# Moving an output projection and re-placing idle matrix products in a windowed-attention kernel

## The reference

```
scores = einsum('bhqd,bhkd->bhqk', q, k) * SCALE
scores = where(|query - key| <= 64, scores, -inf)
out = einsum('bhqk,bhkd->bhqd', softmax(scores), v)
out = out.transpose(0, 2, 1, 3).reshape(B, N, D) @ Wo + bo
```

## Time and profile before

| | |
|---|---|
| median of 3 runs | 2369.12 us (2367.04 to 2376.89) |
| profiled execution | 2362.09 us, span 2360.4 us from the first to the last instruction |
| mean granted TensorE clock | 0.983 |
| busy: PE, PEld, DVE, ACT, POOL | 96%, 90%, 79%, 60%, 12% |
| sampling phase | about 86 to 269 us of the span |
| attention phase | about 324 to 849 us |
| spline phase | about 849 us to the end |
| idle products (L1282) | 248 |

### The profile page before, as it was taken

The page is one execution under the profiler, slowest core; times in us unless marked ns, Lnnn a source line. Parts: engine busy times, 40 slices in busy tenths (PEclk is TensorE's granted clock), DMA queues, the critical chain, the costliest instruction groups (busy, mean ns, idle before and its releaser), DMA issues.

```text
span 2360.4 us, 49109 instructions
## 1 busy us (share of the span) xinstructions
PE 2264.6 (96%) x20033; PEld 2120.2 (90%) x20033; DVE 1873.1 (79%) x2241; ACT 1413.1 (60%) x1391; POOL 295.0 (12%) x169
## 2 busy tenths in 40 slices
PE   6599989999999899999999999999999999999999
PEld 5266777888888799999999999999999999999999
DVE  7699765666666588776776776679999999999996
ACT  6489303444444464534434435499998888888881
POOL 7622100000000022221321321000000000000000
PEclk9799998999999899999999999999999999999999
DMA  6656241111111111111111111221000000000000
GB/s 206 181 147 156 69 159 27 47 47 48 47 48 47 44 32 45 41 51 54 39 50 54 40 49 37 66 80 30 23 23 23 23 23 23 23 23 23 23 19 10
DMA packets 115455, 129.99 MB, mean 55 GB/s; under 512 B 17063, under 2 KB 106167, under 8 KB 115127
## 3 DMA queue, kind: packets, MB, share of 16 engines
q1 hardware_dynamic: 95215, 103.54, 14.6%
q10 hardware_dynamic: 16520, 14.34, 2.1%
q0 software_dynamic: 3616, 10.54, 1.7%
HBM read 92.79 MB, written 35.58 MB: 54 GB/s over the span
## 4 chain that ended last, share of the span: by engine, by line
PE 62%; DVE 2%; ACT 0%; issue 0%; DVEq 0%
PE spline_acc L1994 17%; PE spline_acc L1990 10%; PE spline_acc L1961 10%; PE spline_acc L1964 10%; PE spline_acc L1962 10%; PE spline_acc L1991 5%; PE spline_xT L764 0%; DVE spline_f_high L1725 0%; DVE spline_f L1725 0%; DVE spline_f_low L1725 0%; DVE spline_f L1714 0%; DVE spline_weights_split L1761 0%; DVE spline_b L1731 0%; DVE spline_front L1731 0%; DVE spline_b L803 0%; DVE spline_front L803 0%
## 5 line engine op out<-in xcount | busy, mean ns | idle before, releaser
L1961 PE MATMUL spline_acc<-spline_f,spline_weights_high 128*128 128x328 f32 x1536 | 481.2, 314 | 1.8 <-DVE spline_f L1714 1.8
L1962 PE MATMUL spline_acc<-spline_f,spline_weights_high 128*128 128x328 f32 x1536 | 479.0, 312 | 0.0
L1964 PE MATMUL spline_acc<-spline_f,spline_weights_low 128*128 128x328 f32 x1536 | 465.5, 312 | 0.0
L1994 PE MATMUL spline_acc<-spline_weights,spline_f 128*128 128x192 f32 x1968 | 342.5, 327 | 0.0
L1994 PEld LDWEIGHTS spline_acc<-spline_weights,spline_f 128*128 128x128 f32 x1968 | 316.6, 190 | 0.0
L1990 PE MATMUL spline_acc<-spline_weights_split,spline_f_high 128*128 128x384 f32 x984 | 304.9, 374 | 2.0 <-DVE spline_f L1725 2.0
L1961 PEld LDWEIGHTS spline_acc<-spline_f,spline_weights_high 128*128 128x128 f32 x1536 | 288.3, 188 | 2.2 <-DVE spline_f L1714 1.6
L1962 PEld LDWEIGHTS spline_acc<-spline_f,spline_weights_high 128*128 128x128 f32 x1536 | 288.8, 188 | 0.0
L1964 PEld LDWEIGHTS spline_acc<-spline_f,spline_weights_low 128*128 128x128 f32 x1536 | 286.0, 188 | 0.0
L1991 PE MATMUL spline_acc<-spline_weights_split,spline_f_low 128*128 128x192 f32 x984 | 248.5, 253 | 0.0
L1714 DVE SCALAR_TENSOR_TENSOR spline_f<-spline_front 128x984 fp32r<-128x984 f32 x128 | 150.3, 1215 | 88.7 <-PE spline_acc L1964 86.6
(11 more groups left out here) (240 smaller groups left out, 4924.5 us busy)
## 6 DMA issues: line engine op xcount, KB each, us to landing
spline_front<-pos_scr SPq DMA_DIRECT2D x32, 540.0 KB, 4.3
hid_scr<-spline_hid SPq DMA_DIRECT2D x64, 164.0 KB, 1.8
spline_xn<-hid_scr SPq DMA_DIRECT2D x41, 256.0 KB, 3.1
attend_spread<-rec_scr SPq DMA_DIRECT2D x128, 61.5 KB, 2.1
pix_scr<-spline_front SPq DMA_DIRECT2D x32, 225.0 KB, 3.1
spline_weights_raw<-w SPq DMA_DIRECT2D x1, 6144.0 KB, 21.5
spline_step_to<-w SPq DMA_DIRECT2D x36, 128.0 KB, 2.1
spline_step_from<-w SPq DMA_DIRECT2D x36, 128.0 KB, 2.1
```

The lines of the kernel that those rows point to most:

```text
L1961: nc.tensor.matmul(z, high, x_high, start=start, stop=False)
L1962: nc.tensor.matmul(z, high, x_low, start=False, stop=False)
L1964: last = nc.tensor.matmul(z, low, x_high, start=False, stop=stop)
L1994: last = nc.tensor.matmul(z, rest[:, cols], w2[:, i, r - SETS, :], start=False, stop=stop)
```

## The change

Four things change.

1. In `sample_phase` TensorE issues 70 products of the 128 x 128 identity with itself (fp32, 128 columns, result unread) before the first image.
2. `project_out` and `residual` of the second half move from `q = 0` to `q = 1`. On TensorE the projection then stands after the second quarter's `queries_scores` and before `keys_scores` of `q = 2`; on VectorE the addition stands after the second `maximum`. The first half's stay at `q = 0`.
3. The 4 idle products at `q = 1`, `i = 1` are gone from the 14 pairs after the first.
4. Idle products are added: in the first pair 24 for 18 at `q = 1`, `i = 0`, and 6 new ones at `q = 2`, `i = 1`, ahead of `queries_scores`; in the last pair 6 each at `q = 1`, `2` and `3` of the first half, ahead of `queries_scores`; in `finish` 6 after each of the two `keys_scores`, and 30 for 20 at its end.

```diff
@@ sample_phase, tensor
+            for _ in range(70):
+                nc.tensor.matmul(acc[:, 1, 1, 0:P], c.ident[:], c.ident[:], start=True, stop=True)
             for u in range(2):
                 image(0, u, True)
@@ attend_phase, vector, pair
-                        if q == 0 and not first:
+                        if q == i and not first:
                             residual(tt - 1 if u == 0 else tt, v, i, use(t, (Y_LAST if last else Y)[i]))
@@ attend_phase, tensor, finish
                 for c in range(2):
                     keys_scores(a, u, 1, c, use(t, MAX[0]))
+                    keep_going(6, xb[:, claim(use(t, MIX_LAST[1])), 0:HG * P])
                 for c in range(2):
                     mix(a, u, 1, c, use(t, MIX_LAST[1]))
                 project_out(a - 2, 1, use(t, Y_LAST[1]))
-                keep_going(20, tp[:, 0, 0:HG * P])
+                keep_going(30, tp[:, 0, 0:HG * P])
@@ attend_phase, tensor, pair
                         if first and q == 1 and i == 0:
-                            keep_going(18, xb[:, claim(use(t, X[0])), 0:HG * P])
-                        if q == 1 and i == 1 and more:
-                            keep_going(6 if first else 4, xb[:, claim(use(t, V[0])), 0:HG * P])
+                            keep_going(24, xb[:, claim(use(t, X[0])), 0:HG * P])
+                        if i == 0 and not more and q >= 1:
+                            keep_going(6, xb[:, claim(use(t, X[0])), 0:HG * P])
+                        if q == 1 and i == 1 and first:
+                            keep_going(6, xb[:, claim(use(t, V[0])), 0:HG * P])
+                        if first and q == 2 and i == 1:
+                            keep_going(6, xb[:, claim(use(t, V[0])), 0:HG * P])
                         if nxt:
                             queries_scores(a + 1, w, 1 - i, q)
-                        if q == 0 and not first:
+                        if q == i and not first:
                             project_out(a - 2, i, use(t, Y[i]))
```

## The result

The changed kernel takes 2389.59 us, the median of 12 runs (2377.50 to 2392.37), beside 2368.61 us for the kernel before, 12 runs on the same chip (2362.27 to 2376.89). The ratio is 1.0081, with a 95% interval from 1.0062 to 1.0099: slower by 21.0 us, where +28.6 was forecast. The profiled execution took 2391.96 us, with a span of 2390.3 and a granted clock of 0.981 over the whole of it (before: 2362.1 and 0.983).

The account below looks back on a forecast made before the run. TensorE, busy 96% of the span, was taken as the bound. 35 - 5.3 + 0.9 - 2.0 + 0 = +28.6 us on the median 2369.1 gave 2398 us; likeliest case 2381 to 2424, 8-in-10 range 2359 to 2428.

Parts of the forecast that it names:

- The steady pair's schedule: Second half of each of 14 steady pairs, clock held: idle products and one wait gone, a 1.23 us wait new, 0.0 us.
- ScalarE's cover: Steady pair: second exponential moves back 0.9 us, leaving 1.2 us of cover; rival that ScalarE becomes late: 2375 us, chance 0.05.
- The clock falls in steady pairs: Steady pair's second half: only 32-row products around a 1.2 us wait lower TensorE's clock; forecast case, chance 0.57.
- The rival in which the clock holds: Steady pairs: no falls because the gap is short and a full-array projection follows; sum -6.4, 2363 us, chance 0.27.
- How many, and how dear: Steady pairs: 9 of 14 fall at 3.85 us each, 35 us; ends 0 and 80.
- The rule of the Trainium skill: Steady pairs: only gaps more than twice as long lower the clock, so this term would be 0; kept as a rival.
- The first pair: First attention pair: added idle products thicken the stretch and remove its 5.7 us clock fall, net -5.3 (at worst +0.4).
- The last pair: Last attention pair and `finish`: added idle products cost 2.8, a held clock gives -1.9; net +0.9, between -2 and +5.
- The sampling: Sampling's first image: 70 products raise the clock and remove VectorE's waits of 1.30 and 1.61; -2.0, between -2.9 and +3.
- the forecast's longer case: Sampling's 70 products: each as long as an idle product of 384 columns, making 16 to 32 us in all.
- the clock's term: Steady pairs: cost of clock falls, 9 x 3.85 = 35 us.
- the rival of the 70 products: Sampling: the 70 products run over by 3 to 15 us, clock held; 2369 to 2381 us, chance 0.03 by itself.

## Why the prediction was nearly right, step by step

*The steady pair's schedule* (0.0 allowed 0.2): right. The wait is 1.16 for 1.23, the second quarter starts 2.03 after the first for 2.02, and with the clock held (four products back in the wait) the pair is 29.17 for 29.02. The step from the projection to the keys' scores was taken as 1.88, from the step to the idle products in the kernel before; it is 2.10 (535.61 to 537.71 there), enough for the 0.15. ScalarE's cover was enough: no wait stands for the later exponential. With the clock held that exponential starts 6.20 behind the first quarter for 5.40 before, 0.8 later where 0.9 was forecast, close behind both the store and the keys' scores; the forecast had named the store alone.

*The clock falls in steady pairs*: right, and shown. The moved projection with the empty wait is enough for the falls (2392.06 with this edit alone), and they go away with four full products in that wait (2367.04). That the move is needed for them isn't shown: with the products gone and nothing moved the timed runs are slower too, and the one trace has no fall there. The rival in which the clock holds is out.

*How many, and how dear*: the term was 9 falls, half dear at 5.7 and half cheap at 2.0, 35 us. It was 13 falls, one of 4.1 and twelve of 1.6 us: (33.25 - 29.17) + 12 x (30.8 - 29.17) = 23.6, and with 13 x 0.15 for the order 25.6. Two errors in opposite directions. What I had weighed against falls, the projection right behind the thin stretch, does not prevent them. That it makes them cheap is my reading, from the first pair's fall before (13.7 us low, no projection close behind, 5.7 us of cost) beside these twelve (3.4 us low). It isn't all of it: the first fall meets the same work and is 6.8 us long. In the other twelve the clock doesn't fall before the projection but in it, and the projection with the keys' scores bears it: 3.44 - 2.18 + 1.03 - 0.67 = 1.62. And I had treated falls as independent throws. They are one pattern: a fall lengthens its pair to 30.8 us, and the next one comes 30.7 us after it, so it meets the next pair in nearly the same place (21.4 us into its pair at 481.8, 20.4 at 819.8). Here and in the profile of the steady pairs' edit alone it goes on so up to the last pair, each pair hit alike.

*The rule of the Trainium skill* ("TensorE: Matmul & The Clock Gate", section "Why this matters for your kernels"), which warns of longer gaps only, and by which the prediction took a gap as short as this not to matter: the runs don't agree. Waits of 1.16 us stand ahead of thirteen falls, and a stretch whose only gap was 0.42 us, filled with 32-row products, had them too. The measurement decides.

*The first pair* (-5.3): -5.4, right; the fall at 386 is gone. *The last pair* (+0.9): +0.2, near, but one execution can't price it. The clock doesn't hold there as forecast: it is low for 3.4 us from 853.9 on. And the kernel before was lucky in its profile: the six profiles without the last pair's additions have 46.9 to 50.5 us there, that of the kernel before the shortest, and the six with them 46.5 to 48.4. So the additions may well bring some 2 us there (means of 49.0 and 47.1), which this one pair of profiles doesn't show.

*The sampling* (-2.0): 0.0. The failed term is the length of the 70 products, taken as 14 us, between 5 and 32; it is 17.5. A third of the columns did not make a third of the time: the forecast's longer case at the high clock, 16 us, was the right one, with 1.7 more for its low stretch. The clock is high when they end (the first image takes 5.02 for 8.19), and they give that back by ending 3.6 us late, with one of VectorE's waits still there (1.56 for 1.30). With 52 the gain of 2.2 is there, near what was forecast for it.

*Not foreseen*: +8.8 in the offsets' convolution of the profiled execution, and +1.6 in the spline, where one stretch of 3.4 us at the low clock stands, at 1618.5. The sum on the profiled execution, +28.6 forecast and +29.9 measured, agrees by some luck: without the +8.8 it is +21.1, and the medians differ by 21.0. Against that the forecast was 7.5 too high: the clock's term by 9.4 (35 for 25.6), less the 2.0 that the sampling didn't bring. One sum of the prediction is 1 us off, without weight: the rival of the 70 products comes to 2368 to 2380 by its own terms, not 2369 to 2381.

## What to carry to other kernels

Before idle products are taken out, look at what stands around them with their fill gone: a wait among products of few rows can drop the clock even where it lasts one microsecond, and a full product just behind it did not prevent that here. A fill should be measured in full-array work, not in busy time, and its length measured once on the chip before it is put ahead of a wait that it must not outlast. In a loop a fall of the clock is no single event: check whether its price makes the next one hit the same place.

## What the runs showed of the hardware that was not expected

- *Falls that lock to the loop.* Of thirteen low stretches the last twelve start 30.7 us apart, in pairs of 30.8 us; with two full fill products, or thin ones, the pattern breaks up and pairs of 29.17 stand between those of 30.8 to 32.4. Why the first fall comes at 447.7 and not a pair earlier, at the same work, is open.
- *The same kernel with and without falls.* With the four idle products gone and nothing moved, twelve executions run from 2363.25 us at a mean clock of 0.982 to 2414.84 at 0.959.
- *TensorE waiting for "issue" ahead of the sampling.* The offsets' convolution ran its 128 products without a gap in 16.1 to 16.3 us, in the kernel before and in the kernels with 52 products, with two fill products, with thin ones and with the first pair's additions alone; with gaps it took 24 to 25 us in the changed kernel, in that with four fill products, in the one with all additions, in the steady pairs' edit alone and in the one with only the four products removed. Kernels with most of the change stand in both groups, and one with hardly any of it in the second. The split follows the batches as well: all four profiles of the first batch of experiments have the gaps, and none of the six of the two later batches, which ran on other chips. No kernel has a profile from two of these batches, so kernel and chip can't be told apart here. The start of that phase varies as well, from 53 to 67 us. The changed kernel's timed runs lie in two groups, 2377.5 to 2379.7 and 2386.8 to 2392.4, about as far apart as these gaps are long; that they are the cause isn't shown, since only profiled executions show the phase.
